# A two-layer transformer on one core: the second layer's feed-forward lists written anew

## The reference

```
xn = layernorm(x)                       # x: 8 x 512 x 128, after the first layer
# attention: 4 query heads, 2 key/value heads of 32
h = rmsnorm(xn) ; q, k, v = h@Wq, h@Wk, h@Wv ; q, k = l2norm(q), l2norm(k)
a = x' + gate * (softmax(causal(q k^T * exp(log_temperature))) v) @ Wo        # x' = xn
# feed-forward, three blocks
h = xn
for blk in range(3):
    y = gelu(layernorm(h @ W[2blk] + b) * gamma + beta)
    h = y @ W[2blk+1] + b' + h
x = x + a + h
```

## Time and profile before

| | |
|---|---|
| median of 3 runs | 1337.44 us (1333.65 to 1340.59) |
| profiled execution | 1333.18 us, of it 1331.4 us between first and last instruction |
| first layer | 0 to 1030.57 us |
| group 0: opening and feed-forward / attention and closing | 1030.57 to 1098.92 / 1098.92 to 1181.35 |
| group 1: opening and feed-forward / attention and closing | 1181.35 to 1247.41 / 1247.41 to 1331.4 |
| busy in the whole span | PE 94%, DVE 67%, ACT 57%, POOL 18% |
| mean granted PE clock | 0.977 |

### The profile page before, as it was taken

The page is one execution under the profiler, slowest core; times in us unless marked ns, Lnnn a source line. Parts: engine busy times, 40 slices in busy tenths (PEclk is TensorE's granted clock), DMA queues, the critical chain, the costliest instruction groups (busy, mean ns, idle before and its releaser), DMA issues.

```text
span 1331.4 us, 26756 instructions
## 1 busy us (share of the span) xinstructions
PE 1251.1 (94%) x10540; PEld 994.2 (75%) x10540; DVE 898.6 (67%) x1890; ACT 754.6 (57%) x2033; POOL 239.9 (18%) x235
## 2 busy tenths in 40 slices
PE   6999999999999999999999999999999779867887
PEld 4778877887788778778877887788778556655755
DVE  4885487558756864786488648755865776669665
ACT  5773476357635744674477347635752665656655
POOL 1302600300120011002000300030011770139211
PEclk9999999999999999999999999999999897989889
DMA  7006000500230032004100400140023000000000
GB/s 234 2 27 181 30 2 28 159 9 2 69 125 1 1 103 91 1 3 144 48 2 27 152 17 2 41 153 1 1 80 115 1 0 2 17 17 1 1 10 25
DMA packets 44284, 64.10 MB, mean 48 GB/s; under 512 B 8128, under 2 KB 18368, under 8 KB 43904
## 3 DMA queue, kind: packets, MB, share of 16 engines
q1 hardware_dynamic: 44160, 62.39, 14.8%
HBM read 59.48 MB, written 2.88 MB: 47 GB/s over the span
## 4 chain that ended last, share of the span: by engine, by line
PE 82%; DVE 5%; POOL 4%; ACT 4%; SPq 2%; issue 1%; DMA 1%; POOLq 0%; ACTq 0%; DVEq 0%
PE psum L1161 14%; PE psum L1135 14%; PE psum L1182 12%; PE psum L64 8%; PE psum L1216 8%; PE psum L65 8%; PE psum L66 7%; PE psum L1222 4%; PE psum L1094 2%; PE psum L1140 2%; POOL rn L521 2%; DVE mneg L872 1%; ACT probs L588 1%; PE psum L1186 1%; ACT pt L609 1%
## 5 line engine op out<-in xcount | busy, mean ns | idle before, releaser
L588 ACT ACTIVATE probs<-psum,mneg 128x512 f32<-128x512 f32 (+3 forms) x640 | 330.5, 529 | 156.3 <-DVE mneg L872 143.9
L872 DVE TENSOR_REDUCE mneg<-psum 128x2 f32<-128x1024 f32 (+2 forms) x320 | 254.2, 820 | 143.5 <-PE psum L1140 140.4
L1161 PE MATMUL psum<-ident,probs 128*128 128x128 f32 x1600 | 231.3, 283 | 9.7 <-ACT pt L609 5.7
L863 DVE COPY pt<-psum 128x512 f32<-128x512 f32 x320 | 206.5, 682 | 37.1 <-PE psum L1161 34.5
L1161 PEld LDWEIGHTS psum<-ident,probs 128*128 128x128 f32 x1600 | 179.6, 143 | 42.8 <-issue 23.1
L628 ACT ACTIVATE sg<-psum 128x512 f32<-128x512 f32 x136 | 81.3, 598 | 208.4 <-PE psum L66 208.3
L901 DVE TENSOR_TENSOR sg<-sg,psum 128x512 f32<-128x512 f32 x128 | 87.8, 686 | 95.3 <-ACT sg L628 94.9
L1216 PEld LDWEIGHTS psum<-down,hm 128*128 128x128 f32 x1088 | 139.4, 191 | 9.5 <-DVE hm L910 0.5
L1182 PE MATMUL psum<-pt,v_all 128*64 128x384 f32 (+5 forms) x1088 | 142.6, 412 | 1.0 <-DVE pt L863 1.0
L1216 PE MATMUL psum<-down,hm 128*128 128x128 f32 x1088 | 142.7, 275 | 0.4 <-DVE hm L910 0.4
L466 POOL TENSOR_TENSOR yt<-yt,rrow 128x512 f32<-128x512 f32 x64 | 87.6, 1379 | 293.9 <-DMA rrow<-sums 293.5
(11 more groups left out here) (228 smaller groups left out, 2036.1 us busy)
## 6 DMA issues: line engine op xcount, KB each, us to landing
crow<-weights SPq DMA_DIRECT2D x256, 128.0 KB, 3.0
rrow<-sums SPq DMA_DIRECT2D x128, 128.0 KB, 3.0
gu_raw<-in_gu SPq DMA_DIRECT2D x1, 2176.0 KB, 11.7
x_all<-in_x SPq DMA_DIRECT2D x8, 256.0 KB, 5.3
out_rows<-x_all SPq DMA_DIRECT2D x8, 256.0 KB, 2.3
down<-in_down SPq DMA_DIRECT2D x1, 1088.0 KB, 13.8
wqkv_raw<-in_wqkv SPq DMA_DIRECT2D x1, 896.0 KB, 6.9
wqkv_raw<-in_wqkv SPq DMA_DIRECT2D x1, 512.0 KB, 5.2
```

The lines of the kernel that those rows point to most:

```text
L588: last = act.activation(probs[:, h * HALF + PROB[t]:h * HALF + PROB[t] + w], bank[SCORE_BANK[c] + h][:, o:o + w], ACT.Exp, bias=mneg[:, s] ...
L863: dve.tensor_copy(turned_rows(rnd)[:, s % 2, :, 3 - s // 2, :], bank[TURN_BANK[s]].rearrange("p (j q) -> p j q", q=P)).then_inc(pt_ready, 1)
L872: last = dve.tensor_reduce(mneg_h[:, :, t], psum[:, b:b + 2, o:o + P * (t + 1)], AX, ALU.max, negate=True)
L1161: last = nc.tensor.transpose(bank[TURN_BANK[s]][:, i * P:(i + 1) * P], probs[:, v:v + P], ident[:, :])
```

## The change

The lists of all four engines for the feed-forward stage are written out call by call, in place of loops over the steps.

* The statistics of the second layer's rows are made in the first layer: DVE's `row_stats(b - 1)` in unit 3 of batch b, then POOL's `inv_sqrt1(b - 1)` with six small instructions (two of them powers), which also makes the factor of the root-mean-square norm. Only batch 7's comes after the last unit. Buffers rstd, nmr and rsmall have a place for each batch. The rows of g = 0 to 2 are normed by ACT and those of g = 3 by DVE: in group 0 from the last units on, in group 1 from round 7 of group 0 on. For this the four batches' rooms are laid on other buffers.
* `norm_qk` and the adding back of the rows (`add_rows1`) go from DVE to POOL. `inv_norms` has two powers of 12 numbers a batch in place of four of 6.
* Turned rows go to bank 4 + g mod 2, queries, keys and values to banks 6 and 7. The queries and keys of g = 0 are turned and split within the stage, and the first scores are issued ahead of the last two `lin_out`.
* Turned sums go to bank 5 (SUMS). `turn_sums1` waits for bank 5 to be taken, not for `rest_k`; `weigh_batch` waits for `rest_q` alone; step 1 of the turns waits for the sums' copy.
* The last output rows of group 0 (bank 4) are made inside group 1's list (`last_rows`).

The diff, cut to its core, with runs of calls set on shared lines (`turn_norm`, `lin_in`, `lin_out`, `norm`, `gelu`, `stats1` are the step's parts as named above, with (block, batch)):

```diff
+        room = [v_all[:, :, :].rearrange("p t n -> p (t n)"), room0[:, :], room1[:, :], flat_yt]
...
+        def rows1_bank(g):
+            return bank[4] if g == G - 1 else bank[7]
...
@@ gpsimd
+            def inv_sqrt1(b):
+                s = slice(b * TILES, (b + 1) * TILES)
+                pool.wait_ge(x1_var_ready, b + 1)
+                setup.step(pool.tensor_tensor(rstd[:, s], var[:, s], mhalf[:, s], ALU.pow))
+                pool.tensor_tensor(nmr[:, s], nmean[:, s], rstd[:, s], ALU.mult)
+                setup.step(pool.tensor_tensor(rsmall[:, 1, s], rstd[:, s], rstd[:, s], ALU.mult))
+                setup.step(pool.tensor_tensor(rsmall[:, 1, s], rsmall[:, 1, s], mv[:, s, 1], ALU.mult))
+                setup.step(pool.tensor_scalar(rsmall[:, 1, s], rsmall[:, 1, s], EPS_RMS, None, ALU.add))
+                pool.tensor_tensor(rsmall[:, 0, s], rsmall[:, 1, s], mhalf[:, s], ALU.pow).then_inc(x1_rstd_ready, 1)
             for b in range(B):
...
                 if b == 0:
                     second_layer_weights()
+                else:
+                    inv_sqrt1(b - 1)
+            inv_sqrt1(B - 1)
...
+                def inv_sqrt(k, g):
+                    s = slice((n0 + g) * TILES, (n0 + g + 1) * TILES)
+                    pool.wait_ge(var1_ready, (q * BLOCKS + k) * G + g + 1)
+                    setup.step(pool.tensor_tensor(rstd[:, s], var[:, s], mhalf[:, s], ALU.pow))
                     pool.tensor_tensor(nmr[:, s], nmean[:, s], rstd[:, s], ALU.mult).then_inc(nmr_ready, 1)
-                def inv_norms(k):
-                    g, t = k // TILES, k % TILES
-                    c = slice(t * (H1 + KV1), (t + 1) * (H1 + KV1))
+                def add_rows1(g):
+                    pool.wait_ge(tr1_done[g], q + 1)
+                    pool.tensor_tensor(xn1[g], xn1[g], x_all[:, n0 + g, :, :], ALU.add).then_inc(xr_ready[g], 1)
+                def inv_norms(g, half):
+                    c = slice(half * TILES // 2 * (H1 + KV1), (half + 1) * TILES // 2 * (H1 + KV1))
                     pool.wait_ge(ss1_ready, n0 + g + 1)
+                    pool.tensor_tensor(rn1[:, g, c], ss1[:, g, c], mhalf[:, 0:TILES // 2 * (H1 + KV1)], ALU.pow).then_inc(rn1_ready, 1)
+                def norm_qk(g):
+                    pool.wait_ge(rn1_ready, 2 * (n0 + g) + 2)
+                    rn = rn1[:, g, :].rearrange("p (t h) -> p t h", t=TILES)
+                    setup.step(pool.tensor_tensor(rn[:, :, 0:H1], rn[:, :, 0:H1], temp1[:, 1:2].unsqueeze(1).to_broadcast([P, TILES, H1]), ALU.mult))
+                    qv = qkv1[g][:, :, 0:H1 * HD1].rearrange("p t (h d) -> p t h d", d=HD1)
+                    kv = qkv1[g][:, :, H1 * HD1:QK].rearrange("p t (h d) -> p t h d", d=HD1)
+                    pool.tensor_tensor(qv, qv, rn[:, :, 0:H1].unsqueeze(3).to_broadcast([P, TILES, H1, HD1]), ALU.mult)
+                    kn_v = kn1[g].rearrange("p t (h r d) -> p t h r d", r=H1 // KV1, d=HD1)
+                    for r in range(H1 // KV1):
+                        last = pool.tensor_tensor(kn_v[:, :, :, r, :], kv,
+                                                  rn[:, :, H1:H1 + KV1].unsqueeze(3).to_broadcast([P, TILES, KV1, HD1]), ALU.mult)
+                    last.then_inc(qkn_ready, 1)
+                add_rows1(1); add_rows1(2); inv_sqrt(0, 0); inv_sqrt(0, 1); inv_sqrt(0, 2); inv_norms(0, 0);
+                inv_sqrt(0, 3); inv_norms(0, 1); add_rows1(3); inv_sqrt(1, 0); norm_qk(0); inv_sqrt(1, 1);
+                add_rows1(0); inv_sqrt(1, 2); inv_sqrt(1, 3); inv_norms(1, 0); inv_sqrt(2, 0); inv_sqrt(2, 1);
+                inv_norms(1, 1); inv_sqrt(2, 2); inv_sqrt(2, 3); norm_qk(1)
+                for g in range(2, G):
+                    inv_norms(g, 0)
+                    inv_norms(g, 1)
+                    norm_qk(g)
...
@@ scalar
+                    if b == B - 1 and u == ROWS_AFTER:
+                        act.wait_ge(y_done, ROUNDS0)
+                        norm_rows1(0, 0)
...
+            act.wait_ge(gu_done, B * UNITS)
+            norm_rows1(0, 1)
+            norm_rows1(0, 2)
             load_table(ACT.Gelu)
...
+                take_ht(0); take_ht(2); take_ht(1); take_qkv1(0); norm(0, 0); take_ht(3); norm(0, 1); gelu(0, 0);
+                norm(0, 2); gelu(0, 1); take_qkv1(1); norm(0, 3); gelu(0, 2); take_qkv1(2); gelu(0, 3); norm(1, 0);
+                take_qkv1(3); gelu(1, 0); norm(1, 1); gelu(1, 1); round_q(ROUNDS0 + n0, 1.0); norm(1, 2);
+                norm(1, 3); gelu(1, 2); gelu(1, 3); round_k(ROUNDS0 + n0); norm(2, 0); norm(2, 1); gelu(2, 0);
+                gelu(2, 1); norm(2, 2); norm(2, 3); gelu(2, 2); gelu(2, 3)
...
+                    if q + 1 < GROUPS and r >= 2 * G - 1:
+                        act.wait_ge(rows_ready, n0 + r - 2 * G + 2)
+                        norm_rows1(n0 + G, r - 2 * G + 1)
+                if q + 1 < GROUPS:
+                    act.wait_ge(rows_ready, n0 + G - 1)
+                    norm_rows1(n0 + G, G - 2)
...
@@ vector
+                    if b and u == STATS1_AFTER:
+                        row_stats(b - 1, x_all[:, b - 1, :, :], x1_var_ready)
...
+            dve.wait_ge(acc_done, B)
+            norm_rows1(0, G - 1)
             add_rows(B - 1)
+            dve.wait_ge(x1_ready, B)
+            row_stats(B - 1, x_all[:, B - 1, :, :], x1_var_ready)
...
+                stats1(0, 0)
+                if q:
+                    last_rows()
                     dve.wait_ge(rows_ready, n0)
+                    norm_rows1(n0, G - 1)
+                stats1(0, 1); stats1(0, 2); square_qk(0); stats1(0, 3); add_hidden(0, 0); add_hidden(0, 1);
+                square_qk(1); stats1(1, 0); stats1(1, 1); add_hidden(0, 2); square_qk(2); add_hidden(0, 3);
+                stats1(1, 2); stats1(1, 3); add_hidden(1, 0); add_hidden(1, 1); stats1(2, 0)
                 rest_q(ROUNDS0 + n0, 1.0)
+                stats1(2, 1)
+                add_hidden(1, 2)
                 rest_k(ROUNDS0 + n0)
-
-                def add_attention(g):
+                add_hidden(1, 3); stats1(2, 2); stats1(2, 3); square_qk(3); take_ffn(0); take_ffn(1);
+                row_maxima(ROUNDS0 + n0 * 2, 0); take_ffn(2); take_ffn(3)
...
@@ tensor
+                if s == 1 and rnd > ROUNDS0:
+                    pe.wait_ge(rrow_ready, (rnd - ROUNDS0) // 2)
...
                 pe.wait_ge(spread_ready, n + 1)
-                transpose_rows(bank[7], spread).then_inc(sums_turned, 1)
+                pe.wait_ge(pt_ready, (ROUNDS0 + 2 * n + 2) * (TURNS - 1) - 1)
+                transpose_rows(SUMS, spread).then_inc(sums_turned, 1)
...
+                turn_rows(0); turn_rows(2); turn_rows(1); lin_in(0, 0)
+                if q:
+                    last_rows()
+                project_qkv(0); lin_in(0, 1); turn_rows(3); lin_in(0, 2); project_qkv(1); turn_norm(0, 0);
+                lin_in(0, 3); turn_norm(0, 1); lin_out(0, 0); turn_norm(0, 2); lin_out(0, 1); lin_in(1, 0);
+                project_qkv(2); turn_norm(0, 3); lin_in(1, 1); lin_out(0, 2); project_qkv(3); lin_out(0, 3);
+                turn_norm(1, 0); lin_in(1, 2)
+                pe.wait_ge(qkv1_ready, n0 + G)
                 turn_q(0)
+                lin_in(1, 3); turn_norm(1, 1); lin_out(1, 0); lin_out(1, 1); lin_in(2, 0); turn_norm(1, 2);
+                lin_in(2, 1); turn_norm(1, 3)
                 turn_k(0)
-                def output_rows(g):
+                lin_out(1, 2); lin_out(1, 3); lin_in(2, 2); turn_norm(2, 0); lin_in(2, 3); turn_norm(2, 1);
+                lin_out(2, 0); lin_out(2, 1); turn_norm(2, 2); turn_norm(2, 3)
...
+                pe.wait_ge(qk_lo_ready, (ROUNDS0 + n0) * 2 + 2)
+                for g in range(2):
+                    pe.wait_ge(ffn_ready, n0 + g + 1)
+                score1(0, 0)
+                lin_out(2, 2)
+                lin_out(2, 3)
...
                     if first and g:
+                        turn_sums1(n0 + g - 1)
                         if g + 1 < G:
-                            pe.wait_ge(qk_lo_ready, (ROUNDS0 + n0 + g + 1) * 2 + 2)
-                        elif g == G:
-                            pe.wait_ge(rows_ready, n0 + G - 1)
-                        else:
-                            pe.wait_ge(rows_ready, n0 + g - 1)
-                        turn_sums1(n0 + g - 1)
+                            pe.wait_ge(qk_lo_ready, (ROUNDS0 + n0 + g + 1) * 2 + 1)
                         weigh_batch(g - 1)
                     if not first and g:
-                        pe.wait_ge(rrow_ready, n0 + g)
                         output_rows(g - 1)
-                pe.wait_ge(rrow_ready, n0 + G)
-                output_rows(G - 1)
+            last_rows()
```

More of the change, by code:

```diff
@@ L307, in build @@
         h_ready = sem("h_ready")
+        ffn_done = sem("ffn_done")
+        ffn_ready = sem("ffn_ready")
         stored = sem("stored")
@@ new lines, in _ @@
+                add_rows1(1)
+                add_rows1(2)
+                inv_sqrt(0, 0)
+                inv_sqrt(0, 1)
```

(83 more changed lines are left out.)

339 lines of the change are left out of this document (163 added, 176 removed).

## The result

The changed kernel takes 1293.33 us (median; 1290.25 to 1296.46), the kernel before beside it 1337.49: a ratio of 0.967 (95% interval 0.964 to 0.971). A second set of runs gave 1290.63 us and 0.967 (0.964 to 0.969). The prediction was 1295.5. The profiled execution took 1290.25 us, its span is 1288.4, at a mean clock of 0.988. From here on "the changed kernel" is this one.

The account below looks back on a forecast made before the run. No engine was full in the steps, each a chain through four engines; attention was bound by PE. Gains of 53.3 us less 9.5 for clock and 2 for POOL beside DVE gave 41.8, predicting 1295.5 us, range 1282 to 1312.

Parts of the forecast that it names:

- Part 1: Opening of group 0: first norm at 1041.15, handed to PE at 1042.75 for 1054.04 before; gain 11.3 us.
- Part 2: Group 0's feed-forward steps: PE's 32.6 us plus 1.6 of waits, scores at 1076.9 for 1098.92; with the opening, gain 22.0.
- Parts 3 and 5: Attention of groups 0 and 1: 76.0 to 71.6 us and 74.77 to 70.2, gains of 4.4 and 4.6.
- Part 4: From group 0's last weighing to group 1's first scores: 72.49 us to 50.2, gain 22.3.
- Part 6: Clock in the second layer: of 15.2 us that half clock costs now, 9.5 are kept as a loss.
- Part 7: First layer: seven `row_stats` on DVE hidden behind PE, cost nothing; uncovered 10.2 us.
- Part 8: POOL beside DVE: POOL's SBUF reads hold DVE's squares, giving back 2 us, at worst 10.4.
- GpSimd as the bound: Rival: beyond 6.5 us per `norm_qk`, POOL's chain sets attention; 1310 us at 6.5, about 1353 at 12; chance 0.03.
- Nothing is moved: Rival: PE is busy anyway and gaps reappear between other engines; 1337 us, chance 0.03.
- The case without dips: Rival: PE is fed well enough to keep 2.4 GHz; 9.5 us less, 1286, chance 0.12.

Follow-up runs that it names:

- the second profile: The changed kernel run once more with nothing altered: median 1290.63 us, ratio 0.967 to the kernel before.
- the kernel made for it: Changed kernel with six more 128x512 copies on POOL at the head of each `norm_qk`: 1308.66 us, ratio 0.980 to the kernel before.
- late statistics: Changed kernel with batch 7's statistics and two row additions moved later: 1294.95 us; with ACT's row norms also inside round 8, 1288.11 and 1288.43.

## Why the prediction was right, point by point

Predicted 41.8 us off the profiled execution; it became 42.9 (1333.18 to 1290.25). The stages at full clock were to be 46.3, 71.6, 50.2 and 70.2, with 11.5 us for clock and port on top. That the total came within 1.1 us is in part luck: the misses below go both ways, and the second profile reached the same span with 13.7 us less at half clock and a first layer that ended 4.2 us later.

| us | predicted | changed | again |
|---|---|---|---|
| first layer later by | 0 | 1.6 | 5.8 |
| opening and steps | 46.3 | 47.6 | 46.5 |
| group 0's attention | 71.6 | 72.0 | 72.0 |
| change of groups | 50.2 | 54.9 | 54.0 |
| group 1's attention | 70.2 | 72.5 | 70.7 |
| clock and port | 11.5 | in the rows above | in the rows above |
| sum | 249.8 | 248.6 | 249.0 |

* **Part 1, the opening: mechanism right.** The turn was to come 12.2 us after the first layer and came after 11.9. POOL's order was as laid out: batch 7's factor, two additions, the first root. The size of the gain fits too, where the order is new: without the early statistics the stage is 11 to 12 us longer, a part of which is clock.
* **Part 2, the steps: right.** 34.2 us were predicted and 35.8 measured, of them 5.8 at half clock. PE was to be busy for over 90% and is for 96%. The moved load alone didn't make it: with the old order opening and steps take 67.5, with POOL busy almost without a pause.
* **Parts 3 and 5, attention: right at full clock.** 24.5, 16.1, 15.8, 15.6 for 24.2, 15.9, 15.9, 15.6, and in group 1 72.5 us, or 70.7 in the profile without a dip there, for 70.2. The wait for `rest_k` is gone. The working behind the 15.9 and 15.9 was off all the same: 2.8 us of gaps and 3.3 of clock are already more than the 5.8 to be explained, one of the two gaps lay in the first stretch, the third had none (its excess is what the clock can cost, 1.7), and in its place the second had the 1.4 us for the addition of rows.
* **Part 4, the change of groups: the term somewhat too small.** 54.9 for 50.2. `lin_in(0, 0)` comes 9.8 us after the weighing for 8.3, the first norm 17.2 for 14.0, its turn 20.0 for 16.5, and the scores 34.9 behind that for 33.7. (The 33.7 is called that of part 2, which has 34.2: 0.5 us of the miss is this slip.) The clock, which part 6 carries, can be most of it: 10.2 us at half between 1152 and 1166, in which the weighing alone took 3.73 us (2.15 at full clock, with the row norms in round 8). The kernel with those norms moved has no dip there and takes 49.2; with PE's wait 2.45 us longer, as in the changed kernel, that makes an estimate of 51.6 at full clock, 1.4 above the term.
* **Part 6, the clock: about right in sum.** The 15.2 us of half clock before come from laying out the old lists, which missed by 3 us; the trace bounds them only, at half of 58.0. Half-clock time went from 58.0 to 23.9 us, and 10.2 in the second profile. At half speed 23.9 us cost at most 12.0 and 10.2 at most 5.1, for 9.5 predicted. It was one term for something that differs by 7 us between two profiles of one program, and so it is the bound on how well any of this could be known.
* **Part 7, the first layer: nearly.** At most 1 to 2 us, of 10.2 if uncovered. That it ends anywhere from 1030.1 to 1037.5 in these profiles has other causes too: its first addition of rows alone lies between 157.9 and 163.4.
* **Part 8, the port: not separated.** `norm_qk` was 0.6 us cheaper than predicted. The first product of a pair took 1.34 us for 0.62, and an addition 1.55 for 1.27. On DVE one square of the four in each group was held, by less than the 1.3 us of the sum: 1.25 and 1.45 us where the others take 0.95. The first of them starts inside POOL's product:

```profile
1057.16 1.05 POOL L548 TENSOR_TENSOR v_all<-v_all,rn 128x512 f32<-128x512 f32 x1
1057.77 1.25 DVE L1086 TENSOR_TENSOR room<-room 128x768 f32<-128x768 f32 x1
```

The longest hold was of the smallest instruction: L1059, four numbers a partition, took 1.23 us for 0.17 beside POOL's addition. The Trainium skill (SBUF — State Buffer, Who interferes with whom) says that a `tensor_scalar` can run in a two-port mode, in which it and a GpSimd instruction shut each other out for the whole instruction; this row agrees with it, though it doesn't show the mode. The squares and L1059 lost 2.3 us together in the first profile; what all holds cost at the end wasn't measured.
* **The rivals.** GpSimd as the bound is a real mechanism, met at 6.6 us by the kernel made for it, and in the old order at 2.5. "Nothing is moved" is what the stages show when the old order is kept with the new load on POOL. The case without dips (1286) was nearly reached by the row norms in round 8, with 6.8 us at half.

Where the account by parts was misleading: it gave each part a gain of its own. Undone one at a time from the nearer of the two medians, statistics cost 15.6, the order 30.5, the sums 12.4 and `norm_qk` 4.4 us, together 62.9 for a whole of some 44. Only the sums were tried in both kernels, and stand by themselves. The others are gains of one chain, which had to be laid out whole to be forecast.

What stays open: why late statistics bring no time although their stage is shorter (a dip at the start of attention is what the profiles show; that it follows from the edit is not shown), how much of `norm_qk`'s move is real, and what the old order costs with `norm_qk` on DVE.

## What to carry to other kernels

When a stage is a chain through four engines and none is full, lay the lists against each other before moving work. Here moved work without a new order brought nothing to the stages, for the engine that took it over (POOL) then worked almost without a pause, and the new order, which also puts over a quarter of that engine's work behind the stage, brought 18 to 21 us a group. After such a change, read the first instruction behind each change of stage on every engine: ACT's norms ahead of the copy that PE waited for were the next 6 us of that stage, 2.5 of them wait and the rest perhaps clock. And price an edit of a few microseconds in the stage's own windows, since its time at the end is blurred by a clock that dips in different places from run to run.

## What was not expected of the hardware

* A product on POOL whose second input is broadcast is faster than one with two full inputs here: 1.05 us for 128x512 against 1.27 (row addition) and 1.29 (product).
* A power of twelve numbers a partition takes 2.27 us, on the line through 1.01 for four and 1.32 for six: the cost goes by the number, 0.155 us each, so fewer and larger powers save only the fixed 0.39.
* A DVE instruction of 0.17 us took 1.23 us beside a POOL addition that had started 0.06 us earlier, and 1.22 in the second profile.
* The same program had 23.9 and 10.2 us at half clock in two profiles.
